# A two-layer transformer kernel on one core: turned probabilities copied by ScalarE in the first repetition, its first rotary sums on VectorE, and the first round of turned tiles without scores

## The reference

```
xn = layernorm(x)
s  = attention0(xn)          # 16 query heads, 4 key heads of 128, rotary; window of 64 keys plus the first 32
g  = silu(ffn0(xn))          # ternary weights: groups of 64, rounded to -1, 0, 1 times the group's mean
x  = x + s * g
xn = layernorm(x)
s  = attention1(xn)          # 16 heads of 16, softmax over all 512 keys, biases
g  = silu(ffn1(xn))          # fp16 activations, exact gelu, 1024 hidden
x  = x + s * g
```

## Time and profile before

| | |
|---|---|
| median of 3 runs | 857.14 us |
| the profiled execution, whole | 856.69 us |
| its span, first to last instruction | 854.9 us |
| mean granted TensorE clock | 0.961 |
| PE busy | 788.3 us (92%) |
| DVE busy | 623.3 us (73%) |
| ACT busy | 466.3 us (55%) |
| POOL (GpSimd) busy | 305.4 us (36%) |
| chain that ended last | PE 69%, DVE 15%, issue 8%, ACT 5%, POOL 2%, DMA 1% |

### The profile page before, as it was taken

The page is one execution under the profiler, slowest core; times in us unless marked ns, Lnnn a source line. Parts: engine busy times, 40 slices in busy tenths (PEclk is TensorE's granted clock), DMA queues, the critical chain, the costliest instruction groups (busy, mean ns, idle before and its releaser), DMA issues.

```text
span 854.9 us, 13268 instructions
## 1 busy us (share of the span) xinstructions
PE 788.3 (92%) x4608; PEld 484.9 (57%) x4608; DVE 623.3 (73%) x1655; ACT 466.3 (55%) x946; POOL 305.4 (36%) x260
## 2 busy tenths in 40 slices
PE   4877766998999999999999999999999999999996
PEld 2454545774544766784544766784534666784543
DVE  6968687686875767678875767678975677678952
ACT  4773635244387677324387677324387777323483
POOL 0847554021200888300200888300201988200201
PEclk9978787899999999999999999999999999999998
DMA  8230000217400311008400311008300310008400
GB/s 263 81 81 26 26 0 26 81 61 220 90 3 20 94 56 33 2 1 252 95 3 20 94 57 32 1 1 259 88 3 20 94 32 1 1 6 246 96 3 25
DMA packets 56818, 55.37 MB, mean 65 GB/s; under 512 B 14256, under 2 KB 43312, under 8 KB 56752
## 3 DMA queue, kind: packets, MB, share of 16 engines
q1 hardware_dynamic: 52768, 49.63, 20.4%
q10 hardware_dynamic: 3664, 3.84, 1.6%
q0 software_dynamic: 320, 1.05, 0.4%
HBM read 39.00 MB, written 15.24 MB: 63 GB/s over the span
## 4 chain that ended last, share of the span: by engine, by line
PE 69%; DVE 15%; issue 8%; ACT 5%; POOL 2%; DMA 1%; SPq 0%; POOLq 0%; DVEq 0%; ACTq 0%
PE bank L916 13%; PE bank L1027 6%; PE bank L1013 5%; PE bank L951 5%; PE bank L1218 5%; PE bank L1234 5%; PE bank L1129 5%; PE bank L1157 4%; PE bank L1201 3%; PE bank L994 3%; PE bank L962 2%; PE bank L1206 2%; DVE mx L1587 2%; PE bank L1149 2%; ACT region L757 2%
## 5 line engine op out<-in xcount | busy, mean ns | idle before, releaser
L1587 DVE TENSOR_REDUCE mx<-bank 128x1 f32<-128x512 f32 x256 | 160.9, 685 | 27.0 <-PE bank L1157 22.2
L598 POOL TENSOR_TENSOR region<-region 128x512 f32<-128x512 f32 x80 | 105.9, 1323 | 177.3 <-DVE region L1410 172.6
L916 PE MATMUL bank<-xnT,wrope 128*128 128x512 f32 x320 | 149.9, 612 | 9.5 <-ACT region L740 7.8
L866 ACT ACTIVATE region<-bank 128x512 f32<-128x512 f32 x256 | 133.3, 601 | 32.5 <-PE bank L1206 30.8
L757 ACT ACTIVATE region<-region,nb 128x128 f32<-128x128 f32 x256 | 81.5, 390 | 91.1 <-DVE nb L1417 90.9
L916 PEld LDWEIGHTS bank<-xnT,wrope 128*128 128x128 f32 x320 | 59.4, 196 | 73.1 <-issue 68.5
L594 POOL TENSOR_TENSOR region<-region,sin_sb 128x512 f32<-128x512 f32 x60 | 82.1, 1368 | 31.7 <-ACT region L740 31.1
L627 POOL TENSOR_TENSOR region<-region,bo_bc 128x256 f32<-128x256 f32 x16 | 11.6, 724 | 204.2 <-DVE region L1466 204.2
L951 PE MATMUL bank<-region 128*128 128x128 f32 x512 | 76.7, 297 | 2.8 <-ACT region L752 1.4
L1403 DVE TENSOR_TENSOR region<-bank,cos_sb 128x512 f32<-128x512 f32 x80 | 54.3, 686 | 33.4 <-PE bank L916 33.1
L738 ACT ACTIVATE region<-bank 64x512 f32<-64x512 f32 x80 | 47.5, 594 | 52.3 <-DVE region L1403 38.1
(11 more groups left out here) (142 smaller groups left out, 1342.6 us busy)
## 6 DMA issues: line engine op xcount, KB each, us to landing
wrope<-in_wrope SPq DMA_DIRECT2D x80, 128.0 KB, 2.2
scratch<-region SPq DMA_DIRECT2D x16, 512.0 KB, 4.9
Qp<-scratch SPq DMA_DIRECT2D x56, 128.0 KB, 3.6
Kp<-scratch SPq DMA_DIRECT2D x56, 128.0 KB, 3.9
scratch<-region SPq DMA_DIRECT2D x16, 256.0 KB, 5.3
X<-in_x SPq DMA_DIRECT2D x4, 512.0 KB, 4.1
out<-X SPq DMA_DIRECT2D x16, 128.0 KB, 2.0
VW<-v_rows SPq DMA_DIRECT2D x16, 102.0 KB, 2.8
```

The lines of the kernel that those rows point to most:

```text
L598: nc.gpsimd.tensor_tensor(dst, dst, tiles(sw[:, r % 2, :], i), ALU.add)\
L866: nc.scalar.activation(P1[:, n % 8, :], turned_bank(n)[:, :], ACT.Exp, scale=SCALE1)\
L916: mm = nc.tensor.matmul(misc(b, name)[:, 0:width], lhs(c), xnT[:, c, :], start=(c == 0), stop=(c == DC - 1))
L1587: nc.vector.tensor_reduce(mx1[:, g % 2, column:column + 1], scores_bank(m)[:, :], AX.X, ALU.max)\
```

## The change

Four things are changed together. In the first repetition the copy of the turned probabilities moves from VectorE to ScalarE, behind its exponentials, swaps, tanh and weight copies of the unit. In the first repetition the five sums of the first head group move from GpSimd to VectorE (`rotary_sum`), right behind each product by the sine, and the last three quantising steps of piece 0 move behind them, as does the values' copy one place forward; GpSimd then goes straight to issuing its four weight loads. In every repetition the plain scores of the second layer start one round later (rounds 1 to 7 instead of 0 to 6), so round 0 has none, the six banks start with n = 32, and what VectorE does at fixed m is moved by four tiles. And the second turned row tile goes to another score bank.

```diff
--- before.py
+++ after.py
@@ -41,7 +41,7 @@
 HALF = 4 * HD
 NPAIR = NH // 2
 LEAD = 4 * GH + 20
-WIDE_FROM = 4 * NH - LEAD
+WIDE_FROM = 4 * NH - LEAD + GH
 N_SPILL, N_DEAL = 4, 8
 FIRST = 4 * GH
 MT_SLOTS = (6, 6 + 4 * GH)
@@ -88,7 +88,7 @@
     return order


-PLACED = {"xt": (2, 5), "xh": (3, 0), "qk": (1, 2, 3, 4), "v1": (5, 7), "dup": (2, 2, 2, 2, 3, 4, 2, 3), "down": (4, 1, 2, 3), "mt": (2, 2, 3, 2)}
+PLACED = {"xt": (2, 6), "xh": (3, 0), "qk": (1, 2, 3, 4), "v1": (5, 7), "dup": (2, 2, 2, 2, 3, 4, 2, 3), "down": (4, 1, 2, 3), "mt": (2, 2, 3, 2)}


 LENT = {("rope", 1): 3, ("rope", 2): 4, ("wo1", 1): 3, ("wo1", 2): 4, ("wo1", 3): 5, ("proj", 2): 4, ("proj", 3): 5, ("wo0", 2): 0, ("wo0", 3): 6}
@@ -638,7 +638,7 @@

             pool.wait_ge(tables_loaded, 16 * N_TAB)
             for b in range(B):
-                for r in range(5):
+                for r in range(5) if b else ():
                     rotate(b, r)
                 for t in range(TT) if b else ():
                     add_output(b - 1, t)
@@ -758,6 +758,10 @@
                                          bias=nb0[:, u % 2, i:i + 1], scale=-1.0)\
                         .then_inc(p0_ready.sem, 1)

+            def first_blocks(b, u):
+                act.wait_ge(t_full.sem, t_full.at(b, u + 1))
+                nc.scalar.activation(PT[:, u % 2, :], t_bank[u % 2][:, :], ACT.Copy).then_inc(pt1_ready.sem, 1)
+
             def turned_outputs(b, c):
                 misc_wait(act, b, ("ot", c))
                 nc.scalar.activation(OT0[:, c, :], misc(b, ("ot", c))[:, :], ACT.Copy).then_inc(ot_ready.sem, 1)
@@ -813,6 +817,8 @@
                             turned_weights(2 * TURN_UNITS.index(s) + k)
                     if s == OT_UNIT:
                         turned_outputs(b, 0)
+                    if b == 0 and s:
+                        first_blocks(b, s - 1)
                     if b == 0 and s in PREPARED:
                         prepare(PREPARED[s])
                     for n, k in SPLIT_AT.get(s, ()) if b == 0 else ():
@@ -1262,12 +1268,12 @@
                     for k in range(TT):
                         for hp in range(2):
                             n = 4 * GH * g + GH * k + 2 * hp
-                            first = hp == 0 and n > 0
-                            if first and n + LEAD < 4 * NH:
-                                scores_ahead(n + LEAD)
+                            with_scores = GH <= n < WIDE_FROM
+                            if with_scores and hp == 0:
+                                scores_ahead(n - GH + LEAD)
                             scores_turned(g, k, hp)
-                            if not first and n + LEAD < 4 * NH:
-                                scores_ahead(n + LEAD)
+                            if with_scores and hp == 1:
+                                scores_ahead(n - GH + LEAD)
                             if (k, hp) == (1, 0) and g + 1 < NG:
                                 turn_max(g + 1)
                         if k or g:
@@ -1410,6 +1416,11 @@
                 nc.vector.tensor_tensor(sw[:, r % 2, :], sw[:, r % 2, :], sin_sb[:, :], ALU.mult)\
                     .then_inc(sin_done.sem, 1)

+            def rotary_sum(r):
+                dve.wait_ge(sin_done.sem, r + 1)
+                dst = rotated(0, r)
+                nc.vector.tensor_tensor(dst, dst, tiles(sw[:, r % 2, :], r), ALU.add).then_inc(rope_done.sem, 1)
+
             def mask_and_max(b, u):
                 dve.wait_ge(s_full.sem, s_full.at(b, u + 1))
                 for i in range(NT):
@@ -1482,10 +1493,12 @@
                 times_cos(0, r)
                 if r:
                     times_sin(0, r - 1)
-                if 1 <= r <= 3:
-                    quantise(0, r + 1)
+                    rotary_sum(r - 1)
+            values0(0)
             times_sin(0, 4)
-            values0(0)
+            rotary_sum(4)
+            for k in range(2, 5):
+                quantise(0, k)
             for b in range(B):

                 if b == 0:
@@ -1497,7 +1510,7 @@
                         mask_and_max(b, s)
                         for r in rope_at(s) if s else ():
                             times_cos(b, r)
-                    if 1 <= s <= NKV * TT:
+                    if b and 1 <= s <= NKV * TT:
                         first_blocks(b, s - 1)
                     for kind, i in ffn_at(b, s) if s < NKV * TT else ():
                         (gate if kind == "gate" else times_up)(b, i)
@@ -1610,9 +1623,9 @@
                         negate_max(g)
                     if m == FIRST - 1:
                         values1(1)
-                    if m == 4 * NH - 9:
+                    if m == 4 * NH - 13:
                         outputs1(b, 0)
-                    if m == FIRST + 5 or i == 10 and g >= 2:
+                    if m == FIRST + 5 or i == 6 and g >= 2:
                         max_low(g - 1)
                     if m in FFN_ROWS:
                         ffn_rows(FFN_ROWS.index(m))
```

## The result

The changed kernel takes **844.51 us** (median of 4 runs, 843.55 to 845.54), the kernel before took 857.19 us beside it (857.06 to 857.53): ratio 0.9852, 95% interval 0.9835 to 0.9869. That is 12.7 us faster; the forecast was 8.5. Two later sets gave 845.57 and 842.98 us for the same kernel, beside 856.44 and 856.13 for the kernel before. The profiled execution took 843.55 us, span 841.7 us, mean granted clock 0.971 (before: 856.69, 854.9, 0.961).

What follows compares the result with a forecast made beforehand. VectorE was taken to pace most units of the first repetition's first layer, and row maxima to hold up TensorE in the second layer; gains 2.0 + 4.8 + 1.7 = 8.5 us made 848.6 us, range 844.3 to 853.6.

Steps and rivals of the forecast that it cites:

- Front: First repetition, up to the first mask step: rotary sums on VectorE, quantising steps behind them; 0.35 us lost.
- Unit 0: First layer's first unit: GpSimd's second-head-group products start before the second ternary piece's scales, slowing small steps; 1.0 us lost.
- Unit 1: First layer: VectorE never idle there, so the copy moved to ScalarE counts; 0.6 us gained.
- Units 3 and 4: First layer: VectorE freed of its copy, but ScalarE's preparing step waits instead; gate at 65.1 us, 0.3 us gained.
- Units 5, 8, 10, 12 and 13: First layer: VectorE goes on without idling behind the copy or waits in it for TensorE; 5 x 0.6 = 3.0 us gained.
- Units 14 to 16: End of first layer: ScalarE's copies stand before its weight splits, which VectorE waits for; 0.6 us lost.
- Rounds: Second layer's first two turned rounds, without the wait for a maximum: 5.2 us; 1.2 us gained per repetition, 4.8 in all.
- Clock of the rounds: Second layer, first two repetitions: clock falls behind the wait for maxima cost 3.4 us; half taken, 1.7 us gained.
- held banks: Rival, second layer: four banks hold round 0 as the maxima did; 0.4 us per repetition, no clock gain, 853.5 us; chance 0.10.
- late maxima: Rival, second layer: last maxima run over, TensorE loses a round of up to 2.69 us per repetition; 862.6 us; chance 0.05.
- VectorE was the whole pace: Rival, first layer: the copies not counted count too, 5 us more gained; 843.6 us; chance 0.12.

Runs made afterwards that it cites:

- front_only: The kernel before with only the five rotary sums moved to VectorE and three quantising steps behind them; 857.61 us, ratio 1.0017.
- changed_again: The whole changed kernel measured once more, nothing else changed; 845.57 us, ratio 0.9873 to the kernel before.
- last_copy_pieces: The changed kernel with ScalarE's sixteenth copy of turned probabilities cut into eight pieces; 844.91 us beside 842.98 of the changed kernel.
- changed_third: The whole changed kernel measured again as a control in a later set; 842.98 us, ratio 0.9858 to the kernel before.
- prepare_first: The changed kernel with ScalarE's preparing step of the third unit ahead of its copy; 842.99 us, then 842.45 beside 842.98 of the changed kernel.
- last_copy_early: prepare_first plus ScalarE's weight split of unit 15 put behind the sixteenth copy; 843.78 us beside 842.45 of prepare_first.
- rounds_only: The kernel before with only the second layer's scores one round later; 849.61 us beside 856.44 of the kernel before, ratio 0.9915.
- Part two alone: The kernel before with only the first repetition's turned probabilities copied by ScalarE instead of VectorE; 851.67 us, ratio 0.9946.

## Why the prediction was right, and where not

The direction was right, and so was the mechanism of the rounds. That 844.5 us lies inside the range is in part luck: it is 0.2 us from its end, the changed kernel's 842.98 us of a later set (kernel before: 856.13) lies outside, and 3.4 us of the result come from a place that no step names. By its steps:

- **Front, 0.35 lost.** The fifth sum ended at 28.87 us (29.1 forecast), sums took 0.69 us, the first mask step began at 32.58 us after 32.55 before. The steps are right; the 0.35 us can't be told, since the first mask step of one program moved by up to 2.2 us between profiles.
- **Unit 0, 1.0 lost: mis-sized, 2.1.** 7.46 us in place of 5.35. The chosen middle assumed that only two small steps could be caught. In fact a small step, a multiply with a broadcast scale and a subtraction were, 3.1 us against quiet, of which the kernel before had paid 1.0 already. The Trainium skill (SBUF — State Buffer, section "Who interferes with whom") would have made it 1.9 by its exclusive lock; this case's rows agree with it in 0.17 against 1.29 us, for the slow step ended at 36.17 us, just behind GpSimd's sum at 36.14. That 1.9 and 2.1 lie so near is partly luck: the 1.9 was for two small steps, and one small step and the multiply were caught. The profiles take two values: 2.1 lost in front_only, after, changed_again and last_copy_pieces, 0.9 in changed_third, the two of prepare_first and last_copy_early, where the small step was spared. So the 1.0 was right for half of them.
- **Unit 1, 0.6 gained: measured 1.6** (6.53 after 8.12). The same contention had been in unit 1 before: GpSimd's products moved from beside unit 1 to beside unit 0, and the multiply that took 2.23 us in unit 1 took 1.21. The prediction booked the loss in unit 0 and forgot its other half; front_only, without the copy's 0.6 us, took 7.11. Together units 0 and 1 give -0.5 us, forecast -0.4.
- **Units 3 and 4, 0.3 gained: 0.5**, with just the wait of ScalarE that it described: the copy waited at 56.21 us, the gate came at 65.80 (65.1 forecast). In both profiles the gate's products of unit 3 ran at half clock; where they did not, in rounds_only, the two units were 1.6 us shorter without any edit, a term that the prediction did not have.
- **Units 5, 8, 10, 12 and 13, 3.0 gained: 2.4**, from units 5 (1.35) and 8 (1.1) alone. In the others the 0.6 us was taken up again. In unit 12 VectorE waited 2.27 us for the next scores, after 1.75. In unit 13 its wait of 1.60 us in the copy became one of 1.26 us for ScalarE's tanh, and the gate came 0.94 us sooner behind the mask step; but the split step behind it, for which GpSimd had started first, took 2.00 us in place of 1.22, and the unit ended 0.17 us longer. In unit 10 it was GpSimd: the first small step took the 0.6 us, and the unit was 8.0 us long in both. Before:

```profile
125.49 1.21 DVE L1305 TENSOR_REDUCE H<-w1T 128x16 f32<-128x1024 bf16 x1
126.74 0.34 DVE L1307 TENSOR_SCALAR H<-H 128x16 bf16<-128x16 f32 x1
```

and after:

```profile
122.47 1.21 DVE L1311 TENSOR_REDUCE H<-w1T 128x16 f32<-128x1024 bf16 x1
123.72 0.94 DVE L1313 TENSOR_SCALAR H<-H 128x16 bf16<-128x16 f32 x1
```

  Units 5 and 8 gave more than 0.6 each; in unit 5 the two small steps of the earlier trace rows fell to 0.33 and 0.18 us, by where GpSimd stood, while the multiply behind them rose from 1.23 to 2.17. Unit 8 differs between profiles: 13.8 to 14.4 us in the four with the copy on VectorE, 13.1 to 14.2 in the ten without, so its 1.1 is one pair's.
- **Units 14 to 16, 0.6 lost: 0.4 gained.** VectorE lost another 0.5 us in unit 14, where it waited 2.14 us for ScalarE's part of the split, after 1.06, but the sixteenth tile's copy no longer stood behind its split, which gave 0.9.
- **Rounds, 1.2 per repetition: measured 1.24 and 1.22** in the two repetitions without a fall of the clock before, 5.2 us for the two rounds as counted. Right.
- **Clock of the rounds, 1.7: measured 2.6** (2.73 + 2.30 - 2 x 1.23), out of 3.4 at most. Halving it was too careful: in all ten profiles with the new rounds no fall stood there. The rivals of this part did not come: held banks would have left 0.4 us a repetition, and late maxima would have made the rounds longer than before, not shorter.
- **What the sum lacked** is the clock in the first repetition: it was read behind the stall of the second layer, not behind TensorE's 1.67 us wait at the end of the first, and not inside the first layer. The projection stage had 3.4 us to give, and they are most of the 4.1 us between 848.6 and 844.5. Whether that much comes in each execution is open: the kernel before itself kept its clock in some, to judge by its spread.

The rival "VectorE was the whole pace" gave 843.6 us, near the result and for the wrong reason: the first layer gave 2.8 us in the two profiles, not 7, and of that only the 1.35 us of unit 5 is seen in every profile.

## What to carry to other kernels

List every wait of TensorE of a microsecond or more in one piece, and read the granted clock of the microseconds behind each, before pricing an edit near it; what the clock gives back can exceed the wait. Compare two profiles of a stage only with its granted clock beside the length: the same code took 124.75 us at 0.82 and 122.20 us at 0.87. When an operation moves off an engine, ask at every later wait whether the engine that takes it was the next one late: five equal gains were booked here and two came, and a VectorE instruction beside GpSimd can soak one up by growing. And contention between VectorE and GpSimd moves with the operation that causes it: book the unit that it leaves along with the one that it enters.

## What was not expected of the hardware

The same program ran from 851.2 to 860.6 us in one set on one chip, and the time goes largely with the mean granted clock. In three sets on three chips, the twelve of 49 runs of the kernel before below 853.5 us had 0.972 to 0.976, the fifteen above 857.1 had 0.958 to 0.962. Part two alone, without the 1.67 us wait, had no run above 852.72 us. And the first mask step of one and the same program began at 32.19, 32.58 or 34.38 us, so 2 us of a difference between two profiles can lie ahead of the first product of interest; the stages have to be compared from mask step to mask step.
